# Macaron layer (feed-forward, gated delta-rule attention, feed-forward): the two feed-forward blocks swap their places in the pipeline

## The reference, cut to what matters

```python
def ffn(x):                      # w1 256x1024, w2 1024x256
    return gelu(x @ w1 + b1) @ w2 + b2          # exact gelu

x = x + 0.5 * ffn(layernorm(x))                 # LN1, first block
x = x + attn(layernorm(x))                      # LN2
x = x + 0.5 * ffn(layernorm(x))                 # LN3, second block

def attn(x):                                    # 4 heads of 64
    q, k, v = (silu(causal_conv4(x @ W)) for W in (Wq, Wk, Wv))
    beta = sigmoid(x @ Wb)
    delta = delta_rule(l2norm(q), l2norm(k), v * beta, chunk=32)
    branches = [fir3(v), fir31(v), delta, v]
    w = floor_and_renormalise(softmax(gate_mlp(x, stats(branches), branches) / temp))
    o = sum(w_i * branch_i)
    return rms_norm_per_head(o) @ Wo
```

## Time and profile before

| | us |
|---|---|
| median of 3 runs | 1224.04 (1224.04 to 1238.88) |
| the profiled execution | 1227.37 |
| its span | 1225.7 |
| TensorE busy | 1056.4 |
| VectorE busy | 820.9 |
| ScalarE busy | 549.3 |
| GpSimd busy | 415.6 |

### The profile page before, as it was taken

The page is one execution under the profiler, slowest core; times in us unless marked ns, Lnnn a source line. Parts: engine busy times, 40 slices in busy tenths (PEclk is TensorE's granted clock), DMA queues, the critical chain, the costliest instruction groups (busy, mean ns, idle before and its releaser), DMA issues.

```text
span 1225.7 us, 25639 instructions
## 1 busy us (share of the span) xinstructions
PE 1056.4 (86%) x10348; PEld 784.7 (64%) x10348; DVE 820.9 (67%) x1556; ACT 549.3 (45%) x965; POOL 415.6 (34%) x648
## 2 busy tenths in 40 slices
PE   3778598899988999899988996999988998887838
PEld 2654485378745886488736884478736885477427
DVE  5774267785687767875788666875787667863263
ACT  1154236443374337543475336453475337532322
POOL 7106500671019500681028400681028400870000
PEclk9889699899999999989999999999999999995668
DMA  5040104110040203111040203011040204020000
GB/s 153 1 102 21 34 1 97 25 31 22 18 104 1 53 1 94 28 26 27 19 104 1 52 19 86 18 24 30 18 104 1 52 1 96 9 52 1 1 0 18
DMA packets 82293, 47.45 MB, mean 39 GB/s; under 512 B 57856, under 2 KB 75776, under 8 KB 82176
## 3 DMA queue, kind: packets, MB, share of 16 engines
q1 hardware_dynamic: 82176, 45.82, 16.4%
HBM read 31.12 MB, written 14.68 MB: 37 GB/s over the span
## 4 chain that ended last, share of the span: by engine, by line
PE 57%; DVE 22%; ACT 8%; issue 5%; SPq 3%; POOL 3%; DMA 1%; DVEq 0%; ACTq 0%; POOLq 0%
PE psum L782 12%; PE psum L784 10%; PE psum L783 10%; DVE conv_acc L1363 4%; PE psum L813 4%; DVE arena L1594 3%; PE psum L975 3%; PE psum L960 3%; PE psum L994 2%; PE psum L999 2%; SPq L347 2%; PE psum L1152 2%; ACT arena L582 2%; DVE arena L1596 2%; POOL arena L522 1%
## 5 line engine op out<-in xcount | busy, mean ns | idle before, releaser
L518 POOL TENSOR_TENSOR l_prod<-arena 64x30 f32<-64x30 f32 (+14 forms) x240 | 150.8, 628 | 599.2 <-DMA arena<-l_dram 581.0
L578 ACT ACTIVATE h_f<-psum,b_col 128x512 f32<-128x512 f32 x128 | 88.0, 688 | 216.4 <-PE psum L784 206.4
L522 POOL TENSOR_TENSOR arena<-arena,l_prod 64x30 f32<-64x30 f32 (+14 forms) x240 | 157.3, 655 | 18.8
L782 PE MATMUL psum<-w_hi,h_hi 128*128 128x256 f32 x512 | 152.0, 297 | 9.2 <-DVE h_lo L1343 9.2
L784 PE MATMUL psum<-w_hi,h_lo 128*128 128x256 f32 x512 | 145.2, 284 | 0.0
L783 PE MATMUL psum<-w_lo,h_hi 128*128 128x256 f32 x512 | 145.1, 283 | 0.0
L1081 PE MATMUL psum<-v_shift,fir_w 128*32 128x512 f32 x1152 | 133.6, 604 | 3.6 <-DMA v_shift<-v_dram 3.6
L1363 DVE SCALAR_TENSOR_TENSOR conv_acc<-psum,conv_col,conv_acc 128x511 f32<-128x511 f32 x144 | 107.8, 748 | 33.5 <-ACT conv_acc L603 22.4
L782 PE MATMUL psum<-xt_hi,w_hi 128*128 128x512 f32 x256 | 109.4, 427 | 14.3 <-DVE b_half L1456 7.0
L1342 DVE CAST h_hi<-h_f 128x512 fp32r<-128x512 f32 x128 | 65.3, 510 | 76.6 <-ACT h_f L578 40.1
L782 PEld LDWEIGHTS psum<-w_hi,h_hi 128*128 128x128 f32 x512 | 98.1, 192 | 15.3 <-DVE h_lo L1343 11.1
(11 more groups left out here) (232 smaller groups left out, 2205.6 us busy)
## 6 DMA issues: line engine op xcount, KB each, us to landing
x_in<-in_L_attn_x SPq DMA_DIRECT2D x8, 512.0 KB, 4.0
v_dram<-v_fm SPq DMA_DIRECT2D x8, 512.0 KB, 2.8
v_shift<-v_dram SPq DMA_DIRECT2D x8, 512.0 KB, 5.0
out<-x_tok SPq DMA_DIRECT2D x8, 512.0 KB, 2.9
v_shift<-v_dram SPq DMA_DIRECT2D x8, 511.0 KB, 7.0
v_shift<-v_dram SPq DMA_DIRECT2D x8, 510.0 KB, 9.1
v_shift<-v_dram SPq DMA_DIRECT2D x8, 509.0 KB, 11.6
arena<-in_L_ffn_w SPq DMA_DIRECT2D x2, 1024.0 KB, 7.1
```

The source lines that it names most:

```text
L518: pool.tensor_tensor(prod, l_inv[:, k + 1:, k:k + 1].broadcast_to(shape), l_inv[:, k:k + 1, 0:k].broadcast_to(shape), ALU.mult).then_inc(i ...
L522: pool.tensor_tensor(l_inv[:, k + 1:, 0:k], l_inv[:, k + 1:, 0:k], prod, ALU.add).then_inc(inverted, 1)
L578: act.activation(h_f[:, m % 2, :], bank, ACT.Gelu, bias=b1_col[:, m:m + 1]).then_inc(read, 1)
L782: pe.matmul(dst, a_hi, b_hi, start=first, stop=False, **kw)
```

## The change

The two blocks change places. The filling of the merge and recurrence of pass i is now the second block (banks `upr`, `outr`) of sequence i - 1, whose attention ended in the pass before. The block in the inverse's shadow is the first one (`upw`, `outw`) of sequence j + 1; its input is LN1 (`ln1`) of loaded data. LN3 of sequence i is normalised in the middle of the shadow and transposed at its end (`next`), for the next pass's filling. The head gains a block in its shadow, pass 0 (now called `zero`) has no filling, `last` has no block in its shadow, and the tail has both the filling and the second block of the last sequence. The residuals stand in a ring of three buffers, indexed by the sequence modulo 3, so GpSimd's copy goes; outputs are stored one pass later, and `load_x` waits for that store. The statistics of LN2 are taken at the end of the preceding pass.

The core of the diff:

```diff
--- before.py
+++ after.py
-        x_in = sb("x_in", [P, TILES, C])
-        x1_tok = sb("x1_tok", [P, TILES, C])
-        x2_tok = sb("x2_tok", [P, TILES, C])
+        x_ring = [sb(f"x_ring{n}", [P, TILES, C]) for n in range(3)]
+
+        def rows_of(seq):
+            return x_ring[seq % 3]
...
-        FFN_A = [("upa", (2, 3) + (2,) * (KT - 2)), ("outa", (3, 4))]
+        FFN_R = [("upr", (2, 3) + (2,) * (KT - 2)), ("outr", (3, 4))]
...
+        V_T = [("v_t", (3, 5)), ("f_t", (0, 1, 7, 2))]
+        LN1 = [("ln1", (6, 4))]
+        LN3 = [("ln3", (6, 4))]
+        HALF = [("lhalf", (3, 5))]
+        FFN_W = [("upw", (0, 4) * (KT // 2)), ("outw", (1, 6))]
+        L_OFF = [("at0", (7, 2)), ("at1", (3, 5)), ("lpair", (7, 2))]
         NEXT = [("next", (7, 2))]
+        first = [("first", (2, 6)), ("upr", (2, 0) * (KT // 2)), ("outr", (3, 4)), ("sums", (5, 1))]
+        front = [LN2, V, K, FIR, Q, V_T, LN1, HALF, FFN_W, L_OFF]
+        both = [STATS, LN2, V, STAT, K, LOGIT, FIR, Q, MIX, V_T]
+        ORDER = {"head": sum(front, first),
+                 "zero": sum([MERGE, RECUR] + both + [LN1, HALF, FFN_W, L_OFF, NEXT], []),
+                 "body": sum([MERGE, RECUR, FFN_R] + both + [LN1, HALF, FFN_W, L_OFF, NEXT], []),
+                 "last": sum([MERGE, RECUR, FFN_R] + both + [HALF, L_OFF, NEXT], []),
+                 "tail": sum([MERGE, RECUR, FFN_R, STATS, STAT, LOGIT, MIX, LN3, FFN_W], [])}
...
-                self.next = mode in ("head", "body")
+                self.fill = mode in ("body", "last", "tail")
+                self.ahead = mode in ("head", "zero", "body")
+                self.wide = self.ahead or mode == "tail"
+                self.w = self.j if self.front else i
+                self.keep = mode in ("zero", "body", "last")
...
+            def store_y(seq):
+                sp.wait_ge(y_made, 2 * seq + 2)
+                sp.dma_start(out_v[seq:seq + 1].rearrange("a p t c -> (a p) t c"), rows_of(seq)[:, :, :]).then_inc(y_stored, 16)
+
             def one_pass(at):
+                if at.fill:
+                    store_y(at.i - 1)
+                if at.ahead and at.back:
+                    if at.fill:
+                        sp.wait_ge(y_stored, 16 * at.i)
+                    else:
+                        sp.wait_ge(setup_dve, SETUP_DVE)
+                    load_x(at.j + 1)
                 if at.front:
                     j = at.j
...
+            def add_bias(seq, n, added):
+                x_seq = rows_of(seq)
+                pool.wait_ge(xn_made[n], (1 if n == 0 else 2) * (seq + 1))
+                for t in range(TILES):
+                    last = pool.tensor_tensor(x_seq[:, t, :], x_seq[:, t, :], b2_half[:, :], ALU.add)
+                last.then_inc(added, 1)
+                pool.wait_ge(added, seq + 1)
+
             def one_pass(at):
-                if at.back:
-
-                    pool.wait_ge(y_stored, 16 * at.i + 1)
-                    pool.wait_ge(x1_made, 2 * at.i + 2)
-                    pool.sem_inc(passed, 1)
-                    pool.tensor_copy(x2_tok[:, :, :], x1_tok[:, :, :]).then_inc(x2_begun, 1)
-                    pool.wait_ge(x2_begun, at.i + 1)
+                if not at.back:
+                    x_ready(pool, 0)
+                    add_bias(0, 0, bias1_added)
+                if at.fill:
+                    add_bias(at.i - 1, 2, bias2_added)
...
+                if at.ahead:
+                    x_ready(pool, at.j + 1)
+                    add_bias(at.j + 1, 0, bias1_added)
+                if not at.front:
+                    add_bias(at.i, 2, bias2_added)
...
             def fill(at, steps):
 
-                if at.front:
+                if at.fill:
                     for n in steps:
-                        ffn_step(at, 0, at.j, n)
+                        ffn_step(at, 0, at.i, n)
...
+                    turn_rows(at, "ln1", xn_made[0], j + 2)
+                if at.front:
                     off_diagonal(at, "lhalf")
-                attend_at, pair_at, next_at = 16, 20, len(STEPS) - 4
-                if at.back:
+                if not at.front:
                     for b in range(2):
                         pe.wait_ge(xn_made[2], 2 * i + b + 1)
                         turn_tiles(at, "ln3", b)
+
+                def wide(steps):
+                    if at.wide:
+                        for n in steps:
+                            ffn_step(at, 1, at.w, n)
+
+                wide(range(0, 4))
                 if at.front:
                     attend(at, 0)
-                if at.back:
-                    for n in range(attend_at):
-                        ffn_step(at, 1, i, n)
+                wide(range(4, 16))
                 if at.front:
                     attend(at, 1)
-                if at.back:
-                    for n in range(attend_at, pair_at):
-                        ffn_step(at, 1, i, n)
+                wide(range(16, 20))
                 if at.front:
                     off_diagonal(at, "lpair")
-                if at.back:
-                    for n in range(pair_at, next_at):
-                        ffn_step(at, 1, i, n)
-                if at.next:
-                    turn_rows(at, "next", xn_made[0], j + 2)
-                if at.back:
-                    for n in range(next_at, len(STEPS)):
-                        ffn_step(at, 1, i, n)
+                wide(range(20, 28))
+                if at.keep:
+                    turn_rows(at, "next", xn_made[2], 2 * i + 2)
+                wide(range(28, 32))
...
+                    residual("outr", rows_of(0), rows_of(0), x1_made)
+                    stats(1, rows_of(0))
+                if at.fill:
+                    dve.wait_ge(bias2_added, i)
+                    residual("outr", rows_of(i - 1), rows_of(i - 1), y_made)
...
+                    x_ready(dve, j + 1)
+                    stats(0, rows_of(j + 1))
+                if at.back:
+                    x_seq = rows_of(i)
                     for b in range(2):
                         bank, read = arrive(dve, at, "wo", b)
                         two = slice(2 * b, 2 * b + 2)
-                        link(dve.tensor_tensor(x2_tok[:, two, :], bank.rearrange("p (t c) -> p t c", t=2), x2_tok[:, two, :],
+                        link(dve.tensor_tensor(x_seq[:, two, :], bank.rearrange("p (t c) -> p t c", t=2), x_seq[:, two, :],
                                                ALU.add))
                         dve.sem_inc(read, 1)
+                        if at.ahead and b == 0:
+                            normalise(0, j + 1, rows_of(j + 1))
                         for t in (2 * b, 2 * b + 1):
-                            last = dve.bn_stats(bn[:, t, :], x2_tok[:, t, :])
+                            last = dve.bn_stats(bn[:, t, :], x_seq[:, t, :])
...
+                elif at.ahead:
+                    normalise(0, j + 1, rows_of(j + 1))
+                if at.ahead:
+                    low(0, j + 1, "ln1")
+
+                def normalise_out():
                     dve.wait_ge(std_made[2], i + 1)
                     link(dve.reciprocal(rstd[:, :], std[2]))
                     for t in range(TILES):
-                        last = dve.tensor_scalar(xn_tok[:, t, :], x2_tok[:, t, :], mv[2][:, t, 0:1], rstd[:, t:t + 1],
+                        last = dve.tensor_scalar(xn_tok[:, t, :], rows_of(i)[:, t, :], mv[2][:, t, 0:1], rstd[:, t:t + 1],
                                                  ALU.subtract, ALU.mult)
                         if t % 2:
                             last.then_inc(xn_made[2], 1)
+
+                def wide_split(m):
+                    if at.wide:
+                        split(1, at.w, m)
+
+                if not at.front:
+                    normalise_out()
                     low_rows(2, "ln3")
-                if at.back:
-                    split(1, i, 0)
-                    split(1, i, 1)
+                if at.front:
+                    off_diagonal("lhalf")
+                wide_split(0)
+                wide_split(1)
                 if at.front:
                     attend(0)
-                if at.back:
-                    split(1, i, 2)
-                if at.front:
-                    off_diagonal("lhalf")
-                if at.back:
-                    split(1, i, 3)
-                if at.next:
-                    normalise(0, j + 1, x_in)
-                if at.back:
-                    split(1, i, 4)
+                wide_split(2)
+                wide_split(3)
+                if at.keep:
+                    normalise_out()
+                wide_split(4)
                 if at.front:
                     attend(1)
-                if at.back:
-                    split(1, i, 5)
+                wide_split(5)
                 if at.front:
                     off_diagonal("lpair")
-                if at.back:
-                    for m in range(6, KT):
-                        split(1, i, m)
-                if at.next:
```

(30 more changed lines are left out.)

164 lines of the change are left out of this document (69 added, 95 removed).

## The result

The changed kernel took **1240.05 us** (median of 20 runs, 1232.21 to 1246.29), the kernel before 1226.55 on the same chip (20 runs); the ratio is 1.0097, 95% interval 1.0077 to 1.0118. Slower by 1%: within the 2% that I had called no change, but above my 1221 and just outside the range of 1202 to 1238. A few executions of later sets fell into a slower state; the ratios leave them out, and the traces of a_clear and a_best are of such ones.

The account below looks back on a forecast made before the run. TensorE, busy 86%, was taken as late in a steady pass, the inverse having 3.7 us to spare. Terms +0.5 + 3.0 + 2.2 - 3.6 - 2.5 - 2.2 = -2.6 us gave 1221 against a median of 1224.0; range 1202 to 1238.

Parts of the forecast that it names:

- the same two stalls: TensorE's instruction stalls at 217.45 and 764.47, 6.45 and 8.05 us before the change, expected to stay as they were.
- one more 1232: Rival 3, TensorE's instruction stalls: one stall more than the two expected gives 1232 us; chance 0.07.
- Head: Before the first merge: +0.5 us for the added load, +3.0 for the inverse slowed by splits beside it.
- would end near 143, before the inverse: Head's shadow: TensorE's new feed-forward filling, some 26 us, ends near 143 and the inverse ends later.
- The prediction's other value for the inverse: Head: by the skill's rule of a port lock shared by VectorE and GpSimd, 5.5 us instead of 3.0.
- The early load: Head: `load_x(1)` puts one more issue ahead of the 57 constant loads VectorE waits for, +0.5 us.
- Pass zero: Its merge and recurrence lose the filling and run at about half the granted clock: 44.4 for 42.2, +2.2 us.
- The bodies' shadows: Shadow in zero and five bodies: first feed-forward product 1.65 us earlier, net 0.6 us a pass, 3.6 for six.
- Last and tail: Last has no splits beside its inverse, -2.5 us; the tail's recurrence is filled, 42.2 rather than 44.4, -2.2.
- Rival 2: Merge of five bodies and last: late `y1` copy becomes the wait, 8 to 12 us, 1231; chance 0.18.
- Rival 1: Shadow falls to the inverse's end: six passes gain 3.7 us and not 0.6, 1203; chance 0.17.
- Rival 4: Head: the inverse pays the full 9.8 us and the clock stays low after, +7, 1228; chance 0.05.

Follow-up runs that it names:

- a_clear: Changed kernel plus idle semaphore increments on TensorE (74 at start, 72 in rest of head and pass zero, 183 a pass) to align its program to blocks: 1319.03 us, 1.0744.
- a_best: Changed kernel plus 46 small matrix products a pass, banks of `f_t` and `ln1` swapped, second sequence's load behind the constants: 1209.97 us, 0.9847.
- a_again: The changed kernel measured again, unchanged: 1235.49 us, ratio 1.0066 to the kernel before.
- a_12: Changed kernel plus 12 idle semaphore increments at the start of TensorE's program: 1234.94 us, ratio 1.0036 to the kernel before.
- a_1: Changed kernel plus one idle semaphore increment at the start of TensorE's program: 1235.42 us, ratio 1.0062 to the kernel before.
- a_1_x: a_1 with the second sequence's load behind the constants as well: 1228.33 us, ratio 0.9991 to the kernel before.
- b_255: Kernel before plus 255 instructions (3 increments, 63 small products) ahead of TensorE's first transposes: 1227.00 us, ratio 1.0004 to the kernel before.
- a_split: Changed kernel with the third and fourth `v_shift` load issued only when the first two have landed: 1227.75 us, ratio 1.0005 to the kernel before.
- b_fill: Kernel before plus the same added 32 x 32 products on TensorE as a_fill: 1219.26 us, ratio 0.9926 to the kernel before.
- a_fill_swap: a_fill with the banks of `f_t` back at 0, 1, 6, 4 and `ln1` in 7, 2: 1212.17 us, ratio 0.9876 to the kernel before.
- a_fill: Changed kernel plus 46 products of 32 x 32 a pass on TensorE, aligning its program to blocks: 1217.38 us, ratio 0.9907 to the kernel before.
- a_fill_hit: a_fill plus 36 more small products at the very start of TensorE's program: 1218.22 us, ratio 0.9899 to the kernel before.

## Why the prediction was wrong

Below, "five traces" are those of the changed kernel, a_again, a_12, a_1 and a_1_x, "two" those of the kernel before and b_255.

- **The third stall is the step that failed first.** I wrote "The matmuls from start to each pass's gram products are as many as before ..., so I expect the same two stalls." The matmuls are, the instructions are not: one semaphore instruction fewer by the first body pass, so its gram products stand at place 6 of a block and not 7. a_1, a_1_x and b_255 show in their traces that this moves the block's arrival, a_split that the `v_shift` loads hold it. The case was in my rivals ("one more 1232"), at 0.07; it measured 8.39. It costs less than it lasts: the first body pass took 140.8 and 141.0 us with it and a body pass without a stall 135.4, so +5.6. Why one place moves the block by 7 us or more isn't settled, and that the medians rest on this stall is argued from traces, as a_1's median did not follow.
- **Head:** +3.0 for the inverse stands against +3.4 for the shadow (57.9 in the mean of six traces, 54.5 in three of before), but the agreement is luck. The inverse's way up to the first `x_t` load grew by 1.9 only; the other 1.5 is the new block's end, the wait for bank 6 shown above. I had written that TensorE "would end near 143, before the inverse"; in a_again its last product of the block is at 148.03, and VectorE's additions follow. The prediction's other value for the inverse, 5.5, didn't come either. The early load was +0.5; the weight is 1.5 later and the store 2.0 (means of the table, a_1 and a_1_x left out): under-sized by 1.5. The trace after, with 55.9, showed less than is usual.
- **Pass zero:** its unfilled recurrence is as forecast, the first stretch here (last number but two: the clock), the answer to the earlier trace rows; the tail's filled one is 41.4.

```profile
147.70:192.20 44.50, 36.23 (x374) 30.89 (x375) 16.05 (x47) 10.82 (x22) 0.00 (x0) 0.54 0.04 12
...
1109.10:1150.50 41.40, 41.38 (x493) 36.07 (x494) 21.85 (x50) 12.57 (x25) 0.00 (x0) 0.94 0.04 14
```

  From the merge to the store zero took 72.3 us in five traces and 70.4 in two: +1.9, forecast +2.2. Right. Its shadow, less the stall in it, was 1.0 shorter (forecast 0.6): +0.9 in all.
- **The bodies' shadows, -0.6 a pass:** the second step that failed. A body pass without a stall took 135.4 us in both kernels (21 passes in five traces, eight in two), its shadow 67.7 against 67.5. `low` ended 36.4 us after the store instead of 36.8, so the order of VectorE's list did a part of what I said (I had 35.9), but I hadn't looked at who frees banks 7 and 2 under `f_t`: TensorE waits there 2.1 us a pass. With the banks swapped and no stalls the five took 669.1, 7.0 less than b_fill's.
- **Last and tail:** 129.6 against 131.7 us, 122.1 against 125.0: -2.1 and -2.9, forecast -2.5 and -2.2. Right.
- **Rival 2, the late `y1` copy:** false. The copy comes 1.8 us behind the first product (705.61), half a microsecond later than before, and is no wait: `x12` follows the first product by 2.75 us as it did (694.00 to 696.75).

```profile
705.61 0.69 DVE L1438 COPY v_shift<-psum 32x512 f32<-32x512 f32 x1
```

```profile
706.58 1.10 PE L916 MATMUL psum<-v_shift 32*32 32x32 f32 x58
```

- **Rival 1** (the shadow falls to the inverse's end) did not happen; a_fill_swap, with body shadows of 66.0 in the mean, went a third of the way. **Rival 4** (9.8 for the inverse) did not happen either.

The sum with these sizes: head +5.4, zero +0.9, bodies 0.0, last -2.1, tail -2.9 is +1.3, and the third stall 5.6: 6.9, where 8.1 (a_again) and 11.9 (first set, both by ratio) were measured. Of the 9.5 between this sum and my -2.6 the third stall is 5.6, the bodies 3.0 and the head 1.9; the rest gave 1.0 back. Open stays a_1: by this sum it should be near 1.001 and measured 1.0062. Its trace has the 4 us of the gate sums; in every run they would bring the sum to 1.004, inside the interval (1.0031 to 1.0093), but only six of twenty traces have them. a_1_x, whose load is worth 1 to 2 us by the marks, came 0.7% lower, 8.7 us, on another chip. Runs that aren't profiled may have stalls that a_1's one trace lacks; that wasn't tried.

The Trainium skill (Runtime: NRT & Kernel Launch, "Instruction fetch mechanics") has the streaming of blocks mostly hidden. The traces agree for most blocks and not for these: with four loads of 0.5 MB in flight a block comes 10 us behind the first load's issue, and at places 194 and 195 TensorE had run dry 4.7 to 6.4 us behind it (the five stalls of the two kernels).

## What to carry to other kernels

Count all instructions of an engine that runs long, not its matmuls: beside a recurring burst of DMA like this one of 12 us, an edit that dropped one instruction went with a stall of 8 us that no dependency shows, so look at the instruction queue beside every idle time called "issue". Cut such a burst in two, or place the blocks so that the engine isn't at a block's end when the burst ends. Read what ended the wait, also where the size came out right: the head's +3.4 looked like my +3.0 and was in part another wait. And when a step moves to another bank, ask what the engine that empties the bank does just before. Take a stall's price from passes with and without it: in the body passes 8 us of waiting cost 5 to 6.

## What the runs showed of the hardware that I had not expected

- An idle semaphore increment costs 0.09 us on TensorE (70 ahead of a wait of 2.4 made 6.5 of it), while 46 products of 32 x 32 spread over four waits of a pass cost nothing that shows, and went with a mean granted clock of 0.939 instead of 0.930 (a_fill and the kernel before beside it).
- In pass zero, where TensorE has no filling between the recurrence's short products, the clock stayed at its lower level almost throughout (0.54 in the stretch above), and in the filled one of the pass before the change it was 0.93.
- With the four loads together no block's transfer starts between 2.9 and 9.6 us behind the first load, in any trace: it comes up to 2.9 us behind (0.5 to 2.9 in a_fill_hit, 1.1 in a_again) or at the burst's end, 10 us on. With the loads in two pairs (a_split) it comes 5.6 to 6.7 us behind.
